# Scores and maxima of the first two attention groups taken chunk by chunk inside the projection, with a reordered start and a halved last tile

## The reference, cut to what matters

```python
x = x + xattn(layernorm(x), ctx_1024, pos, pos, Wq, Wkv, Wout, bout)
x = x + ffn(layernorm(x), w_fc, w_proj)

def xattn(x, ctx, pos, ctx_pos, Wq, Wkv, Wout, bout):   # 4 x 512 rows, width 512, ctx width 256, 32 heads of 16
    q = rope(x @ Wq, pos); k, v = split(ctx @ Wkv); k = rope(k, ctx_pos)
    w = softmax(einsum('bqhd,bkhd->bhqk', q, k) / 4)
    return einsum('bhqk,bkhd->bqhd', w, v).reshape(b, n, 512) @ Wout + bout

def bitlinear(x, w):         # ffn = bitlinear, gelu, bitlinear; hidden width 2048
    xn = layer_norm(x)                                   # eps 1e-6
    g = max(|xn|, axis=-1);  x_hat = clip(xn * 128 / g, -128, 128) * g / 128
    gamma = mean(|w|);       w_hat = sign(round(w / (gamma + 1e-6))) * gamma
    return x_hat @ w_hat.T
```

## Time and profile before

| what | us |
|---|---|
| median of 3 runs | 815.09 (814.35 to 815.36) |
| the profiled execution, its own time | 815.23 |
| its span, first to last instruction | 813.3 |
| granted TensorE clock, mean | 0.979 |
| busy PE / DVE / ACT / POOL | 782.3 / 679.5 / 452.3 / 332.6 |

### The profile page before, as it was taken

One profiled execution on the slowest core, in us unless ns is written; L12 is line 12 of the kernel. 1 busy time (PEld: TensorE's weight loads), 2 busy tenths in 40 slices (PEclk: granted clock), 3 DMA queues, 4 the chain that ended last, 5 costly groups with the idle time before them and its releaser, 6 DMA issues.

```text
span 813.3 us, 11712 instructions
## 1 busy us (share of the span) xinstructions
PE 782.3 (96%) x3844; PEld 333.6 (41%) x3844; DVE 679.5 (84%) x940; ACT 452.3 (56%) x828; POOL 332.6 (41%) x428
## 2 busy tenths in 40 slices
PE   3999997999999999999999999899999999999996
PEld 3788884122222222222322232244444444444442
DVE  6888887888888888888888888269999998988983
ACT  5567664277777777777777777734223432233330
POOL 2687776724543554455445544323212211111000
PEclk9999998599999999999999999999999999999999
DMA  7588887545465554667656653325556546553463
GB/s 260 156 221 261 236 227 183 122 110 127 125 170 138 153 145 133 154 142 164 163 155 166 172 167 80 84 64 122 109 123 151 111 90 117 109 125 79 78 130 90
DMA packets 173677, 116.17 MB, mean 143 GB/s; under 512 B 114562, under 2 KB 145330, under 8 KB 173618
## 3 DMA queue, kind: packets, MB, share of 16 engines
q1 hardware_dynamic: 173618, 115.44, 57.0%
HBM read 64.50 MB, written 25.43 MB: 111 GB/s over the span
## 4 chain that ended last, share of the span: by engine, by line
PE 86%; DVE 7%; DMA 2%; ACT 2%; issue 2%; POOL 2%; SPq 0%; DVEq 0%; POOLq 0%; ACTq 0%
PE banks L682 15%; PE banks L669 15%; PE banks L643 13%; PE banks L915 11%; PE banks L279 11%; PE banks L927 10%; PE banks L901 7%; PE banks L304 2%; DVE h_scales L995 1%; DMA stack_words<-max_rows 1%; DVE maxima L713 1%; DVE h_stats L982 1%; ACT probs_words L733 1%; PE banks L264 1%; ACT probs_words L1045 1%
## 5 line engine op out<-in xcount | busy, mean ns | idle before, releaser
L713 DVE TENSOR_REDUCE maxima<-banks 128x2 f32<-128x1024 f32 x256 | 302.0, 1216 | 52.1 <-PE banks L643 52.0
L733 ACT ACTIVATE probs_words<-banks 128x512 f32<-128x512 f32 x512 | 276.0, 597 | 101.3 <-PE banks L669 99.4
L669 PE MATMUL banks<-stack_words 98*128 98x512 bf16 x512 | 175.6, 386 | 2.7 <-ACT probs_words L733 1.8
L643 PE MATMUL banks<-stack_words 96*128 96x512 bf16 x512 | 160.2, 395 | 4.5 <-DVE maxima L713 3.9
L682 PE MATMUL banks<-probs_words,late_words 128*32 128x512 f32 x1024 | 137.2, 608 | 0.5
L927 PE MATMUL banks<-ternary_words,stack_words 128*128 128x512 f16 x512 | 114.6, 383 | 4.5 <-DMA stack_words<-stack_words 4.5
L915 PE MATMUL banks<-ternary_words,late_words 128*128 128x512 f16 x512 | 113.1, 379 | 0.0
L1045 ACT ACTIVATE probs_words<-probs_words,h_moments 128x2048 f32<-128x2048 f32 x16 | 32.0, 2002 | 135.8 <-DVE h_moments L987 135.8
L669 PEld LDWEIGHTS banks<-stack_words 98*128 98x128 bf16 x512 | 39.5, 97 | 144.2 <-ACT probs_words L733 84.3
L747 POOL TENSOR_SCALAR neg_max<-maxima 128x16 f32<-128x16 f32 x32 | 8.3, 258 | 175.0 <-DVE maxima L713 175.0
L927 PEld LDWEIGHTS banks<-ternary_words,stack_words 128*128 128x128 f16 x512 | 50.5, 99 | 70.0 <-issue 13.5
(11 more groups left out here) (129 smaller groups left out, 932.1 us busy)
## 6 DMA issues: line engine op xcount, KB each, us to landing
o_rows<-late_words SPq DMA_DIRECT2D x32, 256.0 KB, 2.8
k_parts<-ternary_words SPq DMA_DIRECT2D x48, 128.0 KB, 3.2
q_parts<-ternary_words SPq DMA_DIRECT2D x48, 128.0 KB, 2.5
stack_words<-q_parts SPq DMA_DIRECT2D x32, 192.0 KB, 3.0
stack_words<-k_parts SPq DMA_DIRECT2D x96, 64.0 KB, 2.7
stack_words<-k_parts SPq DMA_DIRECT2D x32, 192.0 KB, 2.8
attn_words<-in_x_dram SPq DMA_DIRECT2D x16, 256.0 KB, 4.2
probs_words<-in_L_ffn_w_fc_dram SPq DMA_DIRECT2D x16, 256.0 KB, 3.3
```

What stands on the lines that cost most here:

```text
L643: mm = self.nc.tensor.matmul(self.score_slot[j % 2][:, i], self.mem.q_stack[0:STACK, slot, head, c * P:(c + 1) * P], self.mem.k_stack[0:ST ...
L669: self.nc.tensor.matmul(self.mem.banks[:, self.ST_BANK[k]], self.mem.k_stack[0:STACK + 2, slot, head, c * P:(c + 1) * P], self.mem.q_stack ...
L713: dve.tensor_reduce(self.maxima[:, g % 2, 2 * j:2 * j + 2], self.score_slot[j % 2], AX.X, ALU.max).then_inc(self.scores_read, 1)
L733: act.activation(self.probs[:, c, head, :], self.mem.banks[:, self.ST_BANK[k]], ACT.Exp, scale=1 / math.sqrt(HEAD)).then_inc(self.exp_done, 1)
```

## The change

It has three parts. **Start:** k of tile 0 is projected before x is turned (`project_kv` becomes `project_k` and `project_v`); ACT makes the high half of wv before the sines; the high halves of wq are made half on ACT, half on POOL (`weight_high_too`); DVE takes statistics and normalise of tile 1 and the low half of wv earlier, and sines later. **Middle:** the scores of groups 0 and 1 are made as 32 single chunks of 128 x 512, all in bank 7, each waiting until the one before it is read, with 32 single reductions (`early_scores`, `early_maxima`). Three of each go into each of the steps 10 to 18 of the projection (27), five come after. The maxima of group 0 are split, turned, copied and loaded in steps 17 to 19. The attention loop begins with step 2 instead of 1. The stacks of groups 0 to 3 are loaded at SP's steps 8, 10, 13 and 15 instead of 14, 16 and after the last store; the wait for all stores moves from ACT to SP; on POOL the splits and the first staging of v go ahead of the first ternarising. **End:** statistics of the last tile go ahead of the second part of the tile before, and the last tile's centring, maximum, clip, both parts and both transposes are done in two halves of 1024 columns (`clip_last`, `split_last`, `turn_last`); `finish` of tile 13 comes after the first parts, the output scale after the second.

The diff, cut; declarations of semaphores, and waits that only count otherwise, are left out:

```diff
+    def weight_high_too(self, pool, loaded, high, raw, ready):
+        pool.wait_ge(loaded, DMA)
+        pool.tensor_copy(high, raw).then_inc(ready, 1)
...
+        self.early_bank = banks[:, 7]
...
-        if g == 0 and j == 1:
+        if g == self.EARLY and j == 0:
+            pe.wait_ge(self.max_saved, 1)
+        if g == self.EARLY and j == 1:
...
+    def early_scores(self, pe, i):
+        g, head, c = i // (GH * CHUNKS), i // CHUNKS % GH, i % CHUNKS
+        if i % (GH * CHUNKS) == 0:
+            pe.wait_ge(self.stacks_loaded[g], STACK_LOADS)
+        need(pe, self.early_read, i)
+        self.nc.tensor.matmul(self.early_bank, self.mem.q_stack[0:STACK, g, head, c * P:(c + 1) * P],
+                              self.mem.k_stack[0:STACK, g, head, :], start=True, stop=True).then_inc(self.early_ready, 1)
...
+    def turn_first_max(self, pe):
+        pe.wait_ge(self.split_ready, 1)
+        self.nc.tensor.transpose(self.early_max_bank, self.max_parts[:, 0], self.mem.identb[:]).then_inc(self.max_turned, 1)
...
+        if g == 0 and k < 3:
+            pe.wait_ge(self.prj.multiplied[1], TILES)
+            for side in range(2):
+                pe.wait_ge(self.prj.rest_done[side], TILES)
...
+    def early_maxima(self, dve, i):
+        g, at = i // (GH * CHUNKS), i % (GH * CHUNKS)
+        dve.wait_ge(self.early_ready, i + 1)
+        dve.tensor_reduce(self.maxima[:, g, at:at + 1], self.early_bank, AX.X, ALU.max).then_inc(self.early_read, 1)
...
-        pool.wait_ge(self.scores_read, (g + 1) * 2 * GH)
+        if g < self.EARLY:
+            pool.wait_ge(self.early_read, (g + 1) * GH * CHUNKS)
...
+    def turn_last(self, sp, part, half):
+        n, k = TILES - 1, FFN // P // 2
+        r, done = n % 2, self.h_first if part == 0 else self.parts_ready
+        sp.wait_ge(done, n + 1 + half)
+        if part + half == 0:
+            need(sp, self.proj_ready, n - 1)
+        sp.dma_start_transpose(self.hT[:, r, part, half * k:(half + 1) * k], self.h_parts[:, r, part, half * HALF:(half + 1) * HALF]
+                               ).then_inc(self.last_turned[part][half], DMA)
...
+    def clip_last(self, dve):
...
+        for half in range(2):
+            dve.wait_ge(self.h_centred, n + 1 + half)
+            dve.tensor_reduce(self.half_max[:, half:half + 1], halves[half], AX.X, ALU.max, apply_absolute_value=True
+                              ).then_inc(self.halves_read, 1)
+        dve.wait_ge(self.halves_read, 2)
...
+        for half in range(2):
+            dve.tensor_scalar(halves[half], halves[half], scale(2), Q_B, ALU.mult, ALU.min).then_inc(self.last_clipped, 1)
+            dve.wait_ge(self.last_clipped, 1 + half)
+            dve.tensor_scalar(self.h_parts[:, r, 0, half * HALF:(half + 1) * HALF], halves[half], -Q_B, None, ALU.max
+                              ).then_inc(self.h_first, 1)
...
+    def split_last(self, dve):
...
+        for half in range(2):
+            part = self.h_parts[:, r, :, half * HALF:(half + 1) * HALF]
+            dve.wait_ge(self.h_first, n + 1 + half)
+            dve.scalar_tensor_tensor(part[:, 1], halves[half], -Q_B, part[:, 0], ALU.max, ALU.subtract
+                                     ).then_inc(self.parts_ready, 1)
...
-        now = self.h[:, n % H_SLOTS, :]
-        act.activation(now, now, ACT.Identity, bias=self.h_moments[:, n % 2, 0:1], scale=-1.0
-                       ).then_inc(self.h_centred, 1)
+        for now in [self.h[:, n % H_SLOTS, :]] if n < TILES - 1 else self.halves(n):
+            act.activation(now, now, ACT.Identity, bias=self.h_moments[:, n % 2, 0:1], scale=-1.0
+                           ).then_inc(self.h_centred, 1)
...
-                if s in (14, 16):
-                    att.load_stacks(sp, s // 2 - 7)
-            att.load_stacks(sp, 2)
-            att.load_stacks(sp, 3)
+                if s in (8, 10, 13, 15):
+                    att.load_stacks(sp, (8, 10, 13, 15).index(s))
+                if s == TILES + 3:
+                    att.load_max(sp, 0)
+            for pair in range(2):
+                sp.wait_ge(prj.parts_stored[pair], PAIR_STORES * BATCH)
...
+                if 1 <= s - 2 < GROUPS:
+                    att.load_max(sp, s - 2)
                 if within(s - 2, GROUPS):
-                    att.load_max(sp, s - 2)
...
+            prj.project_k(pe, 0)
             prj.turn_x(pe, 0)
-            prj.project_kv(pe, 0)
+            prj.project_v(pe, 0)
...
-                    prj.project_kv(pe, s - 3)
+                    prj.project_k(pe, s - 3)
+                if s == TILES + 2:
+                    att.turn_first_max(pe)
+                if s >= 10:
+                    att.early_scores(pe, 3 * (s - 10))
+                if 1 <= s - 3 < TILES:
+                    prj.project_v(pe, s - 3)
                 if within(s - 4, TILES):
                     prj.turn_rotated(pe, s - 4, 1)
+                if s >= 10:
+                    att.early_scores(pe, 3 * (s - 10) + 1)
                 if within(s - 3, TILES):
                     prj.project_q(pe, s - 3)
-            att.scores(pe, 0, 0)
+                if s >= 10:
+                    att.early_scores(pe, 3 * (s - 10) + 2)
             prj.turn_rotated(pe, TILES - 1, 0)
-            att.scores(pe, 0, 1)
...
             prj.turn_rotated(pe, TILES - 1, 1)
-            att.scores(pe, 0, 2)
+            for i in range(28, att.SINGLES):
+                att.early_scores(pe, i)
+            pe.wait_ge(att.early_read, att.SINGLES)
             prj.add_totals(pe)
-            for j in range(3, 2 * GH):
-                att.scores(pe, 0, j)
-            for s in range(1, GROUPS + 3):
...
+            for s in range(2, GROUPS + 3):
...
             prj.ctx_low(dve, 0)
             prj.normalise(dve, 0)
+            prj.statistics(dve, 1)
+            prj.weight_low(dve, (prj.w_high_ready, 2), prj.wv_sb[1], prj.wv_raw, prj.wv_sb[0])
+            prj.x_low(dve, 0)
             prj.negate_sine(dve)
...
-            prj.weight_low(dve, 2, prj.wv_sb[1], prj.wv_raw, prj.wv_sb[0])
-            prj.x_low(dve, 0)
+            prj.normalise(dve, 1)
             prj.rope_products(dve, 0, 0)
...
                     prj.rope_products(dve, s - 4, 1)
+                if s > 10:
+                    att.early_maxima(dve, 3 * (s - 11) + 2)
...
                     prj.take_first(dve, s - 4, 0)
+                if s >= 10:
+                    att.early_maxima(dve, 3 * (s - 10))
...
                     prj.rope_products(dve, s - 3, 0)
+                if s >= 10:
+                    att.early_maxima(dve, 3 * (s - 10) + 1)
                 if within(s - 4, TILES):
                     prj.take_first(dve, s - 4, 1)
+            prj.rope_products(dve, TILES - 1, 1)
+            att.early_maxima(dve, 26)
+            prj.take_first(dve, TILES - 1, 0)
+            att.early_maxima(dve, 27)
             prj.sum_ffn(dve)
-            prj.rope_products(dve, TILES - 1, 1)
-            att.row_maxima(dve, 0, 0)
-            prj.take_first(dve, TILES - 1, 0)
-            att.row_maxima(dve, 0, 1)
+            att.early_maxima(dve, 28)
             prj.take_first(dve, TILES - 1, 1)
-            att.row_maxima(dve, 0, 2)
+            for i in range(29, att.SINGLES):
+                att.early_maxima(dve, i)
             prj.weigh_ffn(dve)
-            for j in range(3, 2 * GH):
-                att.row_maxima(dve, 0, j)
...
-                if within(s - 3, TILES):
+                if within(s - 3, TILES) and s != TILES:
                     rows.finish(dve, s - 3)
...
+                if s == TILES:
+                    rows.clip_last(dve)
+                    rows.finish(dve, s - 3)
+                    rows.split_last(dve)
...
-                if within(s - 1, TILES):
+                if s == TILES - 1:
+                    rows.statistics(dve, s)
+                if within(s - 1, TILES - 1):
                     rows.second_h(dve, s - 1)
...
-            prj.weight_high(act, prj.w_loaded["wk"], plain(prj.wk_sb[0]), order(prj.wk_raw))
+            prj.weight_high(act, prj.w_loaded["wk"], plain(prj.wk_sb[0]), order(prj.wk_raw), prj.w_high_ready)
             prj.save_ctx(act, 0)
+            prj.weight_high(act, prj.w_loaded["wv"], prj.wv_sb[0], prj.wv_raw, prj.w_high_ready)
             prj.take_sines(act)
-            prj.weight_high(act, prj.w_loaded["wv"], prj.wv_sb[0], prj.wv_raw)
             prj.save_x(act, 0)
-            for k in range(KX):
-                prj.weight_high(act, prj.wq_loaded[k], plain(one(prj.wq_sb[0], k)), order(one(prj.wq_raw, k)))
-                if k == 1:
-                    prj.save_v(act, 0)
-                    prj.save_ctx(act, 1)
+            for k in (0, 2):
+                prj.weight_high(act, prj.wq_loaded[k], plain(one(prj.wq_sb[0], k)), order(one(prj.wq_raw, k)),
+                                prj.wq_high_ready[0])
+            prj.save_v(act, 0)
+            prj.save_ctx(act, 1)
...
-            for pair in range(2):
```

(30 more changed lines are left out.)

99 lines of the change are left out of this document (69 added, 30 removed).

## The result

The changed kernel takes **803.35 us** (median; 801.4 to 805.7), the kernel before, beside it, 814.72: a ratio of 0.986, 95% interval 0.9835 to 0.9885. The profiled execution has a time of its own of 803.88 and a span of 801.8 (before 815.23 and 813.3). The sum of the prediction was 802.0, and its range holds the result; but the terms did not all come out, and the table of stages shows which.

The account below looks back on a forecast made before the run. PE bounds the kernel nearly throughout, so the change works where the chain of waits leaves it. Front -0.5, middle -7.1 (6.8 - 13.9) and end -5.5 sum to -13.1, giving 802.0 us, range 797.5 to 807.5.

Parts of the forecast that it names:

- Sum of the front: -0.5: Start: DVE's new order brings the third statistics and first turned k 0.6 earlier, POOL's copies cost 0.1; ends -1.2 and +1.3.
- Both ways locked: Rival, start: POOL's weight copies hold DVE's first low part, front +0.8 instead of -0.5, 803.3 us; chance 0.08.
- Projection: +6.8: Projection: 26 single scores at 0.22 on PE (5.7) plus 1.1 from DVE delay its end by 6.8; range 5.7 to 10.9.
- DVE becomes the bound by 0.22: Projection steps with three singles: DVE needs 7.95 us, PE 7.73; over five steps this costs +1.1.
- Hand-over: Projection's end to attention: start at 8.7 us instead of 22.6, -13.9, with round trips through one bank exposed for some 1.8.
- First attention step kept at 14.7: Attention: first step stays slow, 14.7 against 11.6 us, TensorE being at 1.2 GHz; 3.1 us kept.
- rival in which attention starts better: Attention's start: clock up after the projection, but group 1's maxima late; 0.5 to 1.8 left, 800.2 to 801.5 us; chance 0.12.
- just in time: Second attention step: group 1's maxima land at E + 22.9 (E: projection's end), needed at E + 23.4; cost 0.
- rival in which ternarising sets the start: Second attention step: group 1's maxima come 2 us later than worked out, POOL being late; 804.0 us; chance 0.08.
- SP's queue: Projection: four earlier stack loads and a wait for stores delay other loads some 5 us; cost 0, at most 1.5.
- End: -5.5: Last tiles: earlier statistics and half transposes let PE go straight on; -6.0, of which -5.5 kept; ends -6.2 and -2.3.
- with the statistics ahead of that split: End: last tile's statistics before DVE's split of tile 14 put its centring at 786.8 instead of 789.15.

Follow-up runs that it names:

- gap filled: Changed kernel with 12 idle transposes of the identity on PE ahead of the wait for the first turned k: 801.82 us, ratio 0.9838.
- early sum: Changed kernel with POOL's sum of the first k products taken right behind its weight copies: 801.68 us, ratio 0.984.
- short reductions: Changed kernel with the early row maxima reading only 256 of 512 scores (part of the computation left out): 800.46 us, one execution.
- two banks: Changed kernel with POOL's first sum earlier and group 1's maxima loaded first, plus the last four single scores alternating between two PSUM banks: 798.8 us, ratio 0.98.
- order only: Changed kernel with the last tile whole again, its statistics still ahead of the second part of tile 14: 808.07 us, ratio 0.9923.
- max first: Changed kernel with the DMA of group 1's maxima issued ahead of the second weight's load: 803.65 us, ratio 0.9868.
- second profile: Changed kernel run and profiled once more, nothing changed, as yardstick: 803.5 us, ratio 0.9855.
- old end: Changed kernel with the whole end of before (last tile unsplit, statistics late, whole transposes): 808.09 us, ratio 0.992.
- old front: Changed kernel with the start put back to the old order, middle and end kept: 802.31 us, ratio 0.9849.

## Why the prediction was right, and where it was not

- **Front: the step that failed.** "Sum of the front: -0.5" counted DVE's instructions and took PE's products at full speed. DVE's part came out as a sum (9.0 us from the second statistics to the third, 9.1 forecast) because small errors cancelled: the lock below cost 0.5 more, and the 0.3 of waits and several tenths of instruction time weren't needed. That the x tile landed at 11.9, near the forecast 11.7, was luck: it lands up to 1.0 later in other executions. In the profiled execution +2.8 came on top, since TensorE ran 6 us at 1.2 GHz; in the second one it was +1.6 (from turned k to M 9.05 against 7.48). The prediction had read a low clock behind sparse work at the hand-over and did not ask the same of the front. With the gap filled M comes at 33.77, 0.6 before that of the kernel before: the gain is there where the clock holds and the tile lands in time.
- **Both ways locked** was put as a rival, and its lock is seen: normalise takes 1.17 us beside GpSimd's copies (two in 2.29) where it takes 0.55 elsewhere (1.13 to 1.18 in all twelve new fronts, 0.55 in the old one, which has no such copies), and GpSimd's tiny L487 takes 1.10 against 0.23 beside DVE's low part. That agrees with what the Trainium skill (SBUF — State Buffer, Who interferes with whom) says of both directions. But the rival's price was wrong: the copies end at 16.92, DVE's first low part starts at 17.17 unhindered, so 0.6 is lost in place of 1.3. The forecast's "as far as the row shows, only POOL waits" does not hold: DVE waits too, and by a whole 1.0 us beside the early sum.
- **The copies** were taken as 1.3 us each; they take 1.15.
- **Projection: +6.8, it was +6.5, but "DVE becomes the bound by 0.22" is wrong.** A reduction takes 0.68, more than the 0.63 assumed, yet DVE's busy time rises by 7.72 - 6.06 = 1.66 in a step, 0.55 for each: back to back, instructions overlap. PE pays 0.23 a product, 3 x 0.23 = 0.69, and sets the step. Two errors cancelled: no 1.1 from DVE, but 6.5 / 26 = 0.25 for each product ahead of E in place of 0.22. The run with short reductions is what shows it.
- **Hand-over: right in its mechanism and size.** The last maximum is read at E + 8.56 (forecast 8.3), attention starts at 9.07 (8.7), the round trips through one bank are exposed as worked out; two banks take 1.4 us back from E to A.
- **First attention step kept at 14.7:** it took 163.21 - 149.73 = 13.5, since the clock is back 5.5 us after the start instead of 8.7. That was luck as well: in the kernels "order only" and "max first" the step took 14.7, and in the changed kernel's second profile it took 13.6, yet A to X was 383.5, no less than before. It is a part of the rival in which attention starts better. What then ends it is the maxima's DMA, which lands at E + 22.5 (forecast 22.9): "just in time" held to 0.4, but on the other side. The rival in which ternarising sets the start was hit in its place, with a price of 0.3 us, not 2.
- **SP's queue, "cost 0":** held; no stage of the projection shows PE waiting for a load.
- **End: -5.5, it was -5.8.** The terms held: split of 14 beside the centring, 0.3 of wait (0.2 said), PE without a pause, half transposes in time (four issues in 5.80 us). That the order alone, with the finish left where it was, would gain nothing was not seen; the statement "with the statistics ahead of that split" reads as a gain of its own and is none. In the medians the end is worth 4.6.

So 802.0 met 803.35 because the large terms, projection (+6.5 for +6.8), hand-over (-13.5 for -13.9) and end (-5.8 for -5.5), were right, and because in the profiled execution an unforeseen loss of 2.8 in front was partly paid by 1.0 from A to X, which the second profile does not repeat, and 0.3 each in the projection and at the end.

## What to carry to other kernels

A start that is sparse on TensorE can have two prices: the pause and what the clock does after it. Count the matmuls behind a pause at both levels. If the pause can't be removed, it can be filled: here that brought 7.5 us in place of 9.1 and 10.3 in the profile, and no difference clear of the noise in the medians. Moving an instruction ahead makes it depend on loads that it did not wait for before; look up how much their landing varies. Where two engines take turns at one PSUM bank, look for a bank whose last reader is done: it was worth 2 us here, from 801.0 to 798.8. And an earlier instruction helps only as far as nothing that waits stands between it and its consumer on the same engine: moving the statistics without the finish gained nothing.

## What was not expected of the hardware

- **The clock's answer to a pause differs between executions.** The same front kept 1.00 behind its pause in one profile (old end) and lost 1.6 to 2.8 us in six; the same pause of 2.35 us was harmless with the old front. What decides is left open. The pause alone does not; nor does it depend only on whether TensorE worked just before, for from 22 to 24 us it was busy throughout (2.00 of 2.00) both with the old front, which kept the clock behind the pause, and in the changed kernel's second profile, which did not.
- **Durations in rows overlap.** Three reductions of 0.69 by their rows take 2.07 when alone, but add only 1.66 to DVE's busy time in a projection step, and three matmuls of 0.39 add 0.69. The price of a short instruction is the distance between starts.
- **A lock seen from the other side:** 0.55 became 1.17 on DVE behind a copy of GpSimd's, and 1.0 became 1.97 to 2.00 beside GpSimd's early sum, with no semaphore between the two.
- **A landing that varies:** the same load of x, among the first of the kernel, let DVE go on at 11.49 us in one execution and at 12.91 in another.
